# Attention of a two-layer block: the value matmuls of two key blocks issued in a row, with four places for the probabilities

## The reference, cut to what matters

```python
# layer 0 (layer 1 has no rotation and its own projections)
q = rope((x @ W_q).reshape(...)); k = rope((lat @ W_uk).reshape(...)); v = (lat @ W_uv).reshape(...)
scores = einsum('bhqd,bhkd->bhqk', q, k) / sqrt(8)
scores = where(causal, scores, -inf)
attn = softmax(scores, axis=-1)
out = einsum('bhqk,bhkd->bhqd', attn, v)
return out.reshape(b, t, 128) @ W_o
```

## Time and profile before

| what | value |
|---|---|
| median of 3 runs | 1483.33 us (1481.02 to 1486.73) |
| the profiled execution's own time | 1480.33 us |
| its span, first to last instruction | 1478.5 us |
| mean granted TensorE clock | 0.882 |
| attention of the first layer | about 80 to 580 us of the span |
| attention of the second layer | about 775 to 1268 us |

### The profile page before, as it was taken

One profiled execution on the slowest core, in us unless ns is written; L12 is line 12 of the kernel. 1 busy time (PEld: TensorE's weight loads), 2 busy tenths in 40 slices (PEclk: granted clock), 3 DMA queues, 4 the chain that ended last, 5 costly groups with the idle time before them and its releaser, 6 DMA issues. The chain is left out here.

```text
span 1478.5 us, 20907 instructions
## 1 busy us (share of the span) xinstructions
PE 1200.0 (81%) x7242; PEld 526.4 (36%) x7347; DVE 938.0 (63%) x2574; ACT 696.4 (47%) x928; POOL 187.7 (13%) x257
## 2 busy tenths in 40 slices
PE   5666899999899997139457899999989999585994
PEld 4322232333233443127332333333323334344663
DVE  6575888888688863101248788888868874442443
ACT  4313456666566665114251364666656667321331
POOL 2220000000000000435320000000000000063442
PEclk8567999999999998559766899999999999687997
DMA  3351000412301000112236011150300000011113
GB/s 128 85 105 33 31 1 26 62 43 35 65 17 58 4 2 1 33 54 65 82 112 106 20 45 33 31 85 2 53 18 2 3 3 2 1 42 40 49 48 105
DMA packets 43908, 63.97 MB, mean 43 GB/s; under 512 B 5672, under 2 KB 32136, under 8 KB 43480
## 3 DMA queue, kind: packets, MB, share of 16 engines
q1 hardware_dynamic: 39496, 53.82, 16.3%
q0 software_dynamic: 4320, 8.92, 1.8%
HBM read 45.42 MB, written 18.92 MB: 44 GB/s over the span
## 5 line engine op out<-in xcount | busy, mean ns | idle before, releaser
L942 ACT ACTIVATE probs_at<-st 128x1024 f32<-128x1024 f32 (+3 forms) x640 | 545.4, 896 | 385.6 <-PE st L897 236.8
L960 DVE TENSOR_REDUCE mxp_at<-mx 128x1 f32<-128x512 f32 x768 | 498.2, 684 | 100.5 <-PE mx L866 93.1
L866 PE MATMUL mx<-ks,qs 128*128 128x512 bf16 (+3 forms) x1218 | 365.8, 366 | 65.9 <-DVEq L951 20.2
L897 PE MATMUL st<-qs,ks 128*128 128x512 bf16 (+3 forms) x1238 | 347.9, 355 | 21.7 <-DMA qs<-shrow_at 15.8
L913 PE MATMUL av<-probs_at,vs 128*32 128x512 f32 (+3 forms) x2560 | 301.0, 542 | 1.1
L962 DVE CUSTOM_DVE_ANT_0 junk_at<-mx,maskN 128x384 f32<-128x384 f32 (+3 forms) x512 | 240.9, 485 | 79.8 <-PE mx L866 76.7
L866 PEld LDWEIGHTS mx<-ks,qs 128*128 128x128 bf16 x1280 | 105.1, 99 | 411.6 <-DVE mxp_at L960 185.0
L897 PEld LDWEIGHTS st<-qs,ks 128*128 128x128 bf16 x1280 | 123.8, 99 | 115.4 <-ACT probs_at L942 21.5
L1177 POOL DMA_INDIRECT perm<-rows,pos x64 | 63.1, 986 | 511.1 <-SPq L1286 248.9
L900 PE MATMUL st<-maskTb,identb 128*128 128x128 bf16 x512 | 101.1, 222 | 0.3
L913 PEld LDWEIGHTS av<-probs_at,vs 128*32 128x32 f32 x2560 | 50.5, 108 | 107.8 <-issue 95.5
(11 more groups left out here) (237 smaller groups left out, 985.7 us busy)
## 6 DMA issues: line engine op xcount, KB each, us to landing
qs<-q_parts SPq DMA_DIRECT2D x63, 128.0 KB
ks<-k_parts SPq DMA_DIRECT2D x18, 384.0 KB
weights<-in_w_dram SPq DMA_DIRECT2D x16, 256.0 KB, 3.0
perm<-in_pad_dram SPq DMA_DIRECT2D x1, 2600.0 KB, 10.9
rows_f<-perm SPq DMA_DIRECT2D x39, 65.0 KB, 1.8
q_parts<-weights SPq DMA_DIRECT2D x9, 256.0 KB, 3.0
rows_f<-perm SPq DMA_DIRECT2D x8, 260.0 KB, 3.0
got_pj<-eo SPq DMA_DIRECT2D x4, 512.0 KB, 7.3
```

The lines of the kernel that those rows point to most:

```text
L866: pe.matmul(buf[:, 0:w], QS[p][:, j, (4 * Q + qb) * P:(4 * Q + qb + 1) * P], KS[p][:, j, c * CH:c * CH + w], start=True, stop=True).then_i ...
L897: mm = pe.matmul(st[half][:, y, off:CH], KS[p][:, j, kb * P:(kb + 1) * P], QS[p][:, j, Q * CH + off:(Q + 1) * CH], start=True, stop=True, ...
L942: act.activation(probs[:, s % 2, 2 * half:2 * half + 2, off:CH], st[half][:, :, off:CH], ACT.Exp, scale=SCALE).then_inc(exp_done[half], 1)
L960: ins = v.tensor_reduce(dst, buf[:, 0:w], AX.X, ALU.max)
```

## The change

In `schedule()` the values of an even step are no longer put right after the next step's scores. They wait for one more step and are then put together with those of the odd step: after the scores of step s, for even s from 2 on, come the values of s-2 and of s-1, and the last two at the end. To allow that, `probs` gets four places instead of two, and the exponential waits for the values of four steps before. To make room in SBUF, `junk` becomes bf16. The number of instructions of every kind stays the same.

```diff
+PBUF = 4
@@ schedule()
             if half == 1:
-                if s:
-                    out.append(("av", s - 1))
-                    pe += 4 * (CH - step_off(s - 1)) / 2400
-                    if s - 1 in LAST:
-                        loaded[LAST.index(s - 1) + 2] = pe + 9
-                    if s in FIRST:
-                        norms.append((pe + 3, "norm", UNIT[s] - 1))
                 s += 1
-                if s == NST:
-                    out.append(("av", NST - 1))
-                    norms.append((pe + 3, "norm", NU - 1))
+                due_av = [s - 3, s - 2] if s % 2 and s > 2 else [NST - 2, NST - 1] if s == NST else []
+                for x in due_av:
+                    out.append(("av", x))
+                    pe += 4 * (CH - step_off(x)) / 2400 + (.1 if x % 2 else .1)
+                    if x in LAST:
+                        loaded[LAST.index(x) + 2] = pe + 9
+                    if x + 1 in FIRST:
+                        norms.append((pe + 3, "norm", UNIT[x]))
@@ attention()
-        probs = sb("probs", [P, 2, GH, CH])
+        probs = sb("probs", [P, PBUF, GH, CH])
-        junk = sb("junk", [P, MXBUF, CH])
+        junk = sb("junk", [P, MXBUF, CH], BF)
@@ values(s), TensorE
-                        mm = pe.matmul(avb[32 * j:32 * j + 32, off:CH], VS[p][:, kb, j, :], probs[:, s % 2, j, off:CH],
+                        mm = pe.matmul(avb[32 * j:32 * j + 32, off:CH], VS[p][:, kb, j, :], probs[:, s % PBUF, j, off:CH],
@@ ScalarE
-                    act.wait_ge(av_done, SB + s + 1)
+                    if SB + s >= PBUF:
+                        act.wait_ge(av_done, 2 + SB + s - PBUF + 1)
```

More of the change, by code:

```diff
@@ L938, in _ @@
                     off = step_off(s)
-                    act.wait_ge(av_done, SB + s + 1)
+                    if SB + s >= PBUF:
+                        act.wait_ge(av_done, 2 + SB + s - PBUF + 1)
                     for half in range(2):
                         act.wait_ge(st_ready[half], SB + s + 1)
-                        act.activation(probs[:, s % 2, 2 * half:2 * half + 2, off:CH], st[half][:, :, off:CH], ACT.Exp,
+                        act.activation(probs[:, s % PBUF, 2 * half:2 * half + 2, off:CH], st[half][:, :, off:CH], ACT.Exp,
                                        scale=SCALE).then_inc(exp_done[half], 1)
```

## The result

The changed kernel takes 1539.98 us in the median (1533.07 to 1540.21, 4 runs) against 1483.56 before: slower by 3.7%, ratio 1.0368, 95% interval 1.0337 to 1.0400. Its profiled execution took 1533.07 us, 52.7 more than the profiled one before.

The account below looks back on a forecast made before the run. The prediction took the chain through VectorE and three `mx` buffers to bound the kernel. Pairs 19.1, runs 1.2 and end 4 us per layer, 48.6 over two, on 1480.33 give 1528.9; it said 1527, range 1493 to 1555.

Parts of the forecast that it names:

- What bounds the kernel: Attention steps: TensorE is nearly full, but the chain setting the step runs through VectorE and three `mx` buffers.
- The chain of 2.87 through VectorE: One attention step, values to values: 0.99 + 0.43 + 0.75 + 0.17 + 0.53 us is 2.87.
- The boundaries: TensorE between scores and values: pairing saves 0.18 us per pair, 29 us over 160 pairs if only TensorE counts.
- VectorE's dry stretch: Pairs with max tiles: 6.07 us against 5.74, 0.33 lost per pair, 19.1 us per layer over 58 pairs.
- Runs of max tiles between units: Four pairs holding 22 or more tiles: even values now follow the run, 0.3 us each, 1.2 per layer.
- The end: Attention's end without max tiles: even scores wait for exponentials, 5.11 us against 4.23 per full pair, about 4 per layer.
- Places and scratch at nothing: Four places of `probs` and bf16 `junk`: cost 0 for the places, gain 0 from the scratch.
- Sum: Whole kernel: 2 x (19.1 + 1.2 + 4) = 48.6 us added over two layers, 1528.9, said as 1527.
- TensorE's busy time down in the attention: Sign in the changed profile: TensorE's busy time falls while the attention lasts about 524 us instead of 500.
- Won boundaries: Rival, chance 0.07: TensorE is the bound, saved boundaries give 1451 us, or 1459 if only 116 pairs gain.
- Cancelling: Rival, chance 0.08: both effects cancel, pairs stay at 5.74 us and the kernel at 1480, give or take 7.4.
- A boundary paid by the second group: Rival, chance 0.07: in each pair the second value group costs 0.18 us more, 1548 to 1556 in all.

Follow-up runs that it names:

- with VectorE short: VectorE reads only 128 columns of each max tile: kernel before with this 1441.7 us, changed kernel with this 1463.17 us.
- both other engines were short: VectorE reads 128 columns per max tile, ScalarE exponentiates half of each tile's columns: kernel before 1443.12 us, changed kernel 1424.62 us.
- Merely moved: Kernel before with four `probs` places and even steps' values moved down to the odd step's, max tiles not planned anew: 1536.01 us, ratio 1.0336.
- after_end_single: Changed kernel, but from step 144 on each step's values follow the next step's scores again, unpaired: 1532.26 us.
- places: Kernel before with four places for `probs` and the bf16 scratch tensor, order unchanged: 1486.63 us, ratio 1.0013.
- the last two runs: pair_apart and after_last_max_late, measured on the same chip, where the kernel before took 1497.53 us: ratios 1.0226 and 1.0263.
- pair_apart: Kernel before with values paired by moving only, but up to three max tiles between the two value groups: 1535.12 us, ratio 1.0226.
- after_last_max_late: Changed kernel with a pair's last max tile put behind the last half of scores, before the values: 1540.73 us, ratio 1.0263.

## Why the prediction was right, point by point

- *What bounds the kernel.* Right. The chain of 2.87 through VectorE was real: taking its 0.09 away by order alone made the kernel faster by 0.9%, and brought the pair to the 5.55 that it takes with VectorE short. TensorE's 76.66 of 78 us busy in the earlier trace rows did not mean that only its own work counts.
- *The boundaries.* Right in kind, under-priced: 1.86 for two groups where I had 1.90, and 0.24 per pair, where I had 0.18, once both other engines were short. They were won and could not be used.
- *VectorE's dry stretch.* Right in its terms, a little too dear: the sum for steps 99 and 100 was 6.07, measured 6.00, with more than half of the difference in the 1.86; the gap was 1.37 where I had about 1.4. So this pair loses 0.26, not 0.33, and one with tiles of 512 alone 0.32 (5.98 to 6.30, steps 103 and 104), not 0.39. Over the dense stretch the mean is 6.92 / 20 = 0.35, close to my 0.33, but by luck: it takes in pairs to which the new plan moved tiles (two more at steps 47 and 48, which lose 1.10).
- *Runs of max tiles between units.* Mis-sized. I had 0.3 each, 1.2 per layer; the one between steps 25 and 33 alone lost 4.0, all of it in steps 31 and 32 (13.41 before, 17.46 now). Merely moved, these two steps took 14.19, so the larger part is the new plan, which has 25 max tiles there and not 21: four tiles of 0.60 on VectorE are 2.4. With VectorE short the same two steps lose 0.8. An execution can differ by about 1 there (16.35 in after_end_single, whose order is the same). I had priced what the values do there, and not that the plan moves tiles into the run. In exchange dense pairs lost 1.1 less in all than under the move alone.
- *The end.* Mis-sized: 4 per layer said, 5.8 measured. The move gives 3.5; the rest comes with the new plan, which by itself costs 0.9 there (after_end_single), and with how the two meet. I take that to be the norms and products that now stand behind a pair of groups where they fill no wait, which no run singles out.
- *Places and scratch at nothing.* Right: 1.0013.
- *Sum.* 48.6 said, 52.7 measured between the profiled executions and 56.4 between the medians: 1527 against 1539.98, inside the range of 1493 to 1555. That the total came so close is partly luck. In the profiled executions the layers lost, between steps 1 and 159, 27.4 and 23.6 us, where I had 24.3 each. Of this the end has 5.8 (I had 4) and steps 31 and 32 have 4.0 and 3.9 (I had 0.3), so what is left for all other pairs and runs is 17.6 and 13.9, where I had 20.0. The pairs were priced too high, the run and the end too low.
- *TensorE's busy time down in the attention.* It can't be read off: 465.26 against 456.50 in the first, but from traces that hold different numbers of its records.
- *The rivals.* Won boundaries: true only with VectorE and ScalarE both short. Cancelling: no. A boundary paid by the second group: no. What I hadn't made clear enough is that there are two floors, one behind the other: ScalarE's 5.76 a pair (measured 5.74) lies not far under VectorE's 6.07 (6.00) and over the 5.55 that two steps take without pairing once VectorE doesn't hold them up, so removing VectorE's part alone would not have saved the change.

## What to carry to other kernels

A switch that costs the busiest engine time is worth removing only if the others can live through the longer stretch that this makes. Add up the chain from the last piece of work handed over to the next one, and compare it with what lies in the buffers: here 3 tiles of 0.6 us against about 3 us of silence. The same sum shows the cheaper way: putting a tile of the other engine's work behind the last half of scores, right before the values, makes the stretch 0.4 us shorter and gained 0.9%.

## What the runs showed of the hardware that was not expected

Between profiled executions two stretches differ although TensorE's order there is the same or nearly so: steps 1 to 9 of the first layer took between 41.2 and 45.2 us, and steps 79 to 89, with the wait for the last group's keys, between 31.4 and 34.8, while the dense stretch repeats to 0.01 us between the kernel before and places. The few us by which runs of one kernel differ have room in those; which wait moves was not traced further. And the kernel before took 1497.53 us on the chip of the last two runs and 1483.56 to 1485.25 on the others, so ratios, not times, compare runs there. In the two traces from that chip 552 and 553 us lie outside steps 1 to 159 of the two layers, in the others 540 to 546, so most of the extra time isn't in the attention; differences of medians would put pair_apart at 1521 and after_last_max_late at 1527 on the first chip.
